# Moving the softmax normalisation of three attentions from VectorE to GpSimd, reading the half maxima as one operand, and swapping two of PE's small uses

## The chip, the cores and the metric

The program runs on one core of one Trainium2 (trn2) chip, as a single launch. The metric is the device time in microseconds (us). Five engines matter: PE (TensorE, matmuls), DVE (VectorE), ACT (ScalarE), POOL (GpSimd), and SP, which only issues the loads and stores here. They run side by side, each takes its own instructions in the order in which they are written, and they wait for each other through semaphores.

## The reference

Two batches of 1024 tokens with 128 features go through eight residual sublayers, each on a layer norm of the running x. Four of the sublayers are attentions with 16 heads of 64. The first (`a0`) has no mask, and its keys and values are shared by the heads; the second (`a1`), the third (`a2`, latent) and the fourth (`a3`, with biases) are causal. The others are quantised linear layers and mixtures of experts. What the change touches is the inner part of an attention:

```python
scores = jnp.einsum('bhsq,bhtq->bhst', q, k)
masked = jnp.where(causal, -jnp.inf, scores)
weights = jax.nn.softmax(masked / jnp.sqrt(jnp.float32(dq)), axis=-1)
out = jnp.einsum('bhst,bhtv->bhsv', weights, v)
return jnp.einsum('bsf,df->bsd', cat, w_o)
```

## The kernel before

**Phases.** `build` runs the phases one after another. `stream_phase` holds `a0` and `a1` in one stream (with the quantised layer between them spread over it), `latent_phase` is `a2`, and `attention_phase` is `a3`. The norms, `moe_phase` and `final_phase` are phases of their own. The change touches `stream_phase` and `attention_phase`, whose inner code is the same but for its bookkeeping.

**Items, steps, units.** An item is a pair of heads and a batch: 16 items in each of `a0`, `a1`, `a3`. An item has two halves of 512 queries (s = 0, 1), each called a unit. A step is one block of 128 keys against one half: 8 + 8 steps per item in `a0`, and 4 + 8 = 12 steps in a causal item (steps 0 to 3 are s = 0, steps 4 to 11 are s = 1; widths shrink on the diagonal). Scores of a step come with keys on the partitions, so the softmax sum over keys is a sum over blocks, made on POOL, and a matmul with ones.

**What one step does.** `scores(g)` on PE: q times k, minus the row maximum (a matmul with `pick`), into one of two buffers of 2 PSUM banks. `exps(g)` on ACT writes the probabilities. `add_up(g)` on POOL adds them into `a.sums`; it skips the first block of a unit, and for the second it waits for PE's `mix_step` of the first. `mix_step(g)` on PE, two steps behind (LAG = 2), multiplies with the values.

**Row maxima, ten steps ahead** (LEAD = 10). `chunk(c)` on PE writes approximate scores of 128 queries against up to 512 keys into the single buffer `chunk_ps`, and `row_max(c)` on DVE reduces it. `chunk(c)` waits for `row_max(c - 1)` (`maxed`), since there is only this one buffer. For more than 512 keys there are two half maxima per query, in `half_max`, of which DVE takes the minimum (they are negated) into `neg_max`.

**Small uses.** One PSUM bank, `small`, is used in turn by everything else on PE. The table `when` gives for each item the step at which each use stands: q, k and v projections, `top` (transpose of `neg_max`, taken by ACT into `max_row`), `total` (ones times `a.sums`, taken by ACT into `a.total`), and `out` (output projection of `a.mixed`, added to `y_t` by DVE). In a causal item each of the 12 steps has exactly one use. PE works in iterations of two steps:

```python
for g in range(BEGIN, LAST, 2):
    chunk(g + LEAD); scores(g); scores(g + 1); chunk(g + 1 + LEAD)
    the use of step g; mix_step(g - 2); mix_step(g - 1); the use of step g + 1
```

**From total to out.** After `total` at step t of a unit, DVE does four `invert` (reciprocals of 128 columns each) at steps t + 1 to t + 4, and `normalise` at step t + 5, ahead of the reciprocal of the same step: `a.mixed` = `a.mixed_raw` times `a.inverse`, 128x512 each. `out` follows. There is one `a.inverse` and one `a.mixed`. So the first `invert` of a unit waits until the unit before has been normalised (semaphore `normed`), and ACT's copy into `a.total` waits for the fourth reciprocal of the unit before (`inverted`). On DVE a step g is: `row_max(g + LEAD)`, then `normalise`, then `invert`, then pieces of the quantised layer; on POOL it is `add_up(g - 1)`, then the rounding copies of q and k (`round_off`).

**Lines.** In the trace of before: `stream_phase`: scores L979, L982, L987; chunk L1003, L1009; mix L1022; total L1057; out L1061; exps L1111; row_max L1194; minimum L1201; reciprocals L1214; normalise L1222; quantised layer L1237 to L1306; POOL's copies L1351 and sums L1361. `attention_phase`: row_max L687, minimum L694, reciprocals L707, normalise L715, sums L772. `latent_phase` already normalises on POOL (L1694).

Of the kernel before, what the change touches and what calls it, by code (L numbers as in the profile page):

```python
# [27 lines left out]
P = 128  # L28
# [18 lines left out]
QUARTERS = 4  # L47
# [330 lines left out]
def attention_phase(nc, m, a, tag, dram, after, causal, biased=False, shared=False):  # L378
# [5 lines left out]
    with phase(nc) as (ctx, new_sem):  # L384
# [48 lines left out]
        if causal:  # L433
            when = {("top", 0): -6, ("top", 1): 2, ("total", 0): 7, ("out", 0): 13, ("total", 1): 15, ("out", 1): 22}
            when |= {("q", 0): -15, ("q", 1): -12}
            if not shared:
                when |= {("k", 0): -16, ("k", 1): -13, ("v", 0): -8, ("v", 1): -7}
        else:
            when = {("top", 0): -2, ("top", 1): 6, ("total", 0): 11, ("out", 0): 18, ("total", 1): 19, ("out", 1): 26}
            when |= {("q", 0): -15, ("q", 1): -12}  # L440
# [231 lines left out]
        def _(dve):  # L672
            v = nc.vector

            def row_max(c):
                i, (t, part, lo, hi) = c // NS, chunks[c % NS]
                s = t // TPG
                dve.wait_ge(chunked, c + 1)
                if split_max[s]:
                    out = a.half_max[:, part, t % TPG, :]  # L680
                    if part == 0 and t % TPG == 0 and unit(i, s) > 0:
                        dve.wait_ge(max_ready, unit(i, s))
                else:
                    out = a.neg_max[:, s, t % TPG, 0:P:HD]
                    if t % TPG == 0 and i >= 1:
                        dve.wait_ge(small_mm, use_of["top", i - 1, s] + 1)
                last = v.tensor_reduce(out, chunk_ps[:, :, 0:hi - lo], AX.X, ALU.max, negate=True)  # L687
                last.then_inc(maxed, 1)
                if c % NS == last_chunk[s]:
                    if split_max[s]:  # L690
                        if i >= 1:
                            dve.wait_ge(small_mm, use_of["top", i - 1, s] + 1)
                        dve.wait_ge(maxed, c + 1)
                        v.tensor_tensor(a.neg_max[:, s, :, 0:P:HD], a.half_max[:, 0], a.half_max[:, 1], ALU.min)\  # L694
                            .then_inc(max_ready, 1)
# [37 lines left out]
            inverts_at, norms_at = {}, {}  # L733
            for i in range(ITEMS):
                for s in range(2):
                    at = i * NS + when["total", s] + 1
                    for quarter in range(QUARTERS):
                        inverts_at[at + quarter] = (i, s, quarter)
                    norms_at[at + QUARTERS] = (i, s)
            for g in range(BEGIN, LAST + 1):  # L740
                if 0 <= g + LEAD < TOTAL:
                    row_max(g + LEAD)
                if g in norms_at:
                    normalise(*norms_at[g])
                if g in inverts_at:
                    invert(*inverts_at[g])
# [5 lines left out]
        def _(pool):  # L752
# [53 lines left out]
def stream_phase(nc, m, a, dram, after):  # L806
# [6 lines left out]
    with phase(nc) as (ctx, new_sem):  # L813
# [74 lines left out]
        def when(i):  # L888
            if layer_of(i)["causal"]:
                at = {("top", 0): -6, ("top", 1): 2, ("total", 0): 7, ("out", 0): 13, ("total", 1): 15, ("out", 1): 22,  # L890
# [286 lines left out]
        def _(dve):  # L1177
# [3 lines left out]
            def row_max(c):  # L1181
# [15 lines left out]
                if ends and split:  # L1197
# [3 lines left out]
                    v.tensor_tensor(a.neg_max[:, s, :, 0:P:HD], a.half_max[:, 0], a.half_max[:, 1], ALU.min)\  # L1201
# [13 lines left out]

            def normalise(i, s):
                u = unit(i, s)
                dve.wait_ge(inverted, QUARTERS * (u + 1))
                dve.wait_ge(mixed_out, u + 1)
                if u >= 1:  # L1220
                    dve.wait_ge(small_mm, use_of["out", (u - 1) // 2, (u - 1) % 2] + 1)
                v.tensor_tensor(a.mixed[:], a.mixed_raw[:, u % 2, :], a.inverse[:], ALU.mult).then_inc(normed, 1)  # L1222
# [85 lines left out]
            inverts_at, norms_at = {}, {}  # L1308
            for i in range(ITEMS):
                for s in range(2):  # L1310
                    at = begins[i] + when(i)["total", s] + 1
                    for quarter in range(QUARTERS):
                        inverts_at[at + quarter] = (i, s, quarter)
                    norms_at[at + QUARTERS] = (i, s)
# [7 lines left out]
            for g in range(BEGIN, LAST + 1):  # L1322
# [6 lines left out]
                if g in norms_at:  # L1329
                    normalise(*norms_at[g])  # L1330
                if g in inverts_at:
                    invert(*inverts_at[g])
# [4 lines left out]
        def _(pool):  # L1337
# [24 lines left out]

            for g in range(BEGIN, LAST + 1):
                if 0 <= g - 1 < TOTAL and step(g - 1)[2] > 0:
                    add_up(g - 1)
                for n, kind, i, part in uses_at.get(g, ()):
# [648 lines left out]
```

## Time and profile before

| | |
|---|---|
| median of 3 runs | 2778.26 us (2777.01 to 2779.09) |
| the profiled execution's own time | 2777.25 us |
| its span | 2775.5 us |
| PE busy | 2530.6 us (91%) |
| PE weight loads | 1243.0 us (45%) |
| DVE busy | 1736.8 us (63%) |
| ACT busy | 1134.6 us (41%) |
| POOL busy | 1237.8 us (45%) |
| mean granted PE clock | 0.945 of full |

The span is what the hardware profiler saw of one execution on the core; the execution's own time is 1.75 us longer, and is what the runs report. Roughly, by the trace: `stream_phase` runs from 45 to 1465 us, `latent_phase` from 1525 to 1880 us, `attention_phase` from 2050 to 2665 us. The shares are averages over all phases. A busy PE is not a PE at its peak, since matmuls overlap; an idle time in front of a PE row, with the engine that ended it, is time in which PE had nothing to run.

### The profile page before, as it was taken

The numbers are of one execution on the slowest core, as the hardware profiler recorded it, in microseconds if no ns is written. First come the engines' busy times: TensorE is split into PE (matmuls) and PEld (weight loads), VectorE is DVE, ScalarE is ACT, GpSimd is POOL, SyncE is SP. The second block draws the span as 40 slices with busy tenths as digits, with TensorE's granted clock in tenths as the row PEclk, the third lists the DMA queues.
The fourth block names the chain that finished last, engine by engine and source line by source line (L and its number), as shares of the span: only waits on it lengthen the run. The fifth ranks groups of instructions, "written<-read, shape, count | busy, mean of one in ns | idle before, by whom it ended". The sixth has DMA issues, their size and how long they took to land. (4 is left out here: it accounts for less than half of the span.)

```text
span 2775.5 us, 47142 instructions
## 1 busy us (share of the span) xinstructions
PE 2530.6 (91%) x19425; PEld 1243.0 (45%) x19425; DVE 1736.8 (63%) x2244; ACT 1134.6 (41%) x1454; POOL 1237.8 (45%) x810
## 2 busy tenths in 40 slices
PE   4999999889999999999994799998869999999968
PEld 2333344333334444444442466665434444444433
DVE  2677767777765766666657467775434666666653
ACT  1444444434444434444441244444214444444422
POOL 2677777666775444555550000000003555555510
PEclk9999999999999999999995699999868999999969
DMA  4000000000000000000000100000000000000000
GB/s 104 1 1 1 1 1 0 1 1 1 1 1 10 1 1 1 1 1 1 1 1 0 32 3 3 3 3 2 0 1 1 1 1 1 1 1 1 1 1 16
DMA packets 19321, 13.99 MB, mean 5 GB/s; under 512 B 3234, under 2 KB 17954, under 8 KB 18979
## 3 DMA queue, kind: packets, MB, share of 16 engines
q1 hardware_dynamic: 19106, 10.97, 1.6%
q8 instruction: 155, 2.54, 0.4%
q14 instruction: 60, 0.48, 0.1%
HBM read 9.39 MB, written 1.57 MB: 4 GB/s over the span
## 5 line engine op out<-in xcount | busy, mean ns | idle before, releaser
L1361 POOL TENSOR_TENSOR sums<-sums,p 128x1024 f32<-128x1024 f32 (+3 forms) x384 | 815.2, 2123 | 389.9 <-PE ps L1022 342.6
L1194 DVE TENSOR_REDUCE half_max<-ps 128x2 f32<-128x1024 f32 (+3 forms) x384 | 440.2, 1146 | 334.9 <-PE ps L1003 322.4
L1111 ACT ACTIVATE p<-ps 128x1024 f32<-128x1024 f32 (+3 forms) x384 | 347.8, 917 | 228.3 <-PE ps L982 163.3
L979 PE MATMUL ps<-q,k 64*128 64x512 f32 (+3 forms) x1792 | 428.0, 556 | 0.0
L772 POOL TENSOR_TENSOR sums<-sums,p 128x1024 f32<-128x1024 f32 (+3 forms) x160 | 276.9, 1731 | 196.1 <-PE ps L545 179.5
L1022 PE MATMUL ps<-p,v 128*64 128x512 f32 (+3 forms) x1536 | 343.8, 562 | 0.0
L982 PE MATMUL ps<-max_row,pick 64*128 64x512 f32 (+3 forms) x896 | 327.2, 726 | 0.0
L1214 DVE RECIPROCAL inverse<-total 128x128 f32<-128x128 f32 x256 | 240.0, 940 | 17.0 <-ACT total L1147 13.2
L1003 PE MATMUL ps<-k_near,q_near 64*128 64x512 f32 (+2 forms) x896 | 201.0, 445 | 51.8 <-DVE half_max L1194 51.7
L687 DVE TENSOR_REDUCE half_max<-ps 128x2 f32<-128x1024 f32 (+3 forms) x128 | 129.2, 1010 | 122.7 <-PE ps L526 107.5
L1003 PEld LDWEIGHTS ps<-k_near,q_near 64*128 64x128 f32 x896 | 85.9, 188 | 265.0 <-issue 157.2
L1578 ACT ACTIVATE p<-ps 128x2048 f32<-128x2048 f32 (+1 forms) x80 | 136.6, 1707 | 161.3 <-PE ps L1483 90.5
L979 PEld LDWEIGHTS ps<-q,k 64*128 64x128 f32 x1792 | 162.9, 187 | 57.1 <-issue 42.1
L1022 PEld LDWEIGHTS ps<-p,v 128*64 128x64 f32 x1536 | 98.0, 139 | 193.5 <-issue 127.1
L1631 DVE TENSOR_REDUCE quarter_max<-ps 128x2 f32<-128x1024 f32 (+3 forms) x128 | 128.3, 1012 | 60.3 <-PE ps L1507 34.8
L502 PE MATMUL ps<-q,k 64*128 64x512 f32 (+3 forms) x768 | 164.8, 507 | 0.0
L611 ACT ACTIVATE p<-ps 128x1024 f32<-128x1024 f32 (+3 forms) x160 | 118.6, 767 | 66.1 <-PE ps L510 49.5
L707 DVE RECIPROCAL inverse<-total 128x128 f32<-128x128 f32 x128 | 119.6, 940 | 15.8 <-ACT total L652 12.3
L982 PEld LDWEIGHTS ps<-max_row,pick 64*128 64x128 f32 x896 | 85.9, 188 | 90.2 <-issue 85.2
L1694 POOL TENSOR_TENSOR mixed<-mixed_raw,inverse 128x256 f32<-128x256 f32 x32 | 23.3, 728 | 229.5 <-DVE inverse L1649 229.5
L505 PE MATMUL ps<-max_row,pick 64*128 64x512 f32 (+3 forms) x384 | 122.1, 632 | 0.0
L1111 ACT ACTIVATE sums<-ps 128x1024 f32<-128x1024 f32 x64 | 65.6, 1025 | 128.6 <-PE ps L982 109.8
(260 smaller groups left out, 3990.5 us busy)
## 6 DMA issues: line engine op xcount, KB each, us to landing
q_w<-in_wq SPq DMA_DIRECT2D x3, 512.0 KB
o_w<-in_wo SPq DMA_DIRECT2D x3, 512.0 KB
k_w<-in_wk SPq DMA_DIRECT2D x2, 512.0 KB
v_w<-in_wv SPq DMA_DIRECT2D x2, 512.0 KB
out<-x SPq DMA_DIRECT2D x4, 256.0 KB, 2.9
scratch<-in_wq_t SPq DMA_DIRECT2D x1, 512.0 KB, 5.4
scratch<-in_w_out SPq DMA_DIRECT2D x1, 512.0 KB, 7.6
gate<-in_gate SPq DMA_DIRECT2D x1, 320.0 KB
```

Source lines behind the costliest of these rows:

```text
L502: nc.tensor.matmul(out[:, head, 0:width], a.k[rows, key_slot(i, 3), k * P:(k + 1) * P], a.q[rows, i % 3, s * BANK + lo:(s + 1) * BANK], st ...
L687: last = v.tensor_reduce(out, chunk_ps[:, :, 0:hi - lo], AX.X, ALU.max, negate=True)
L772: pool.tensor_tensor(sums, sums, probabilities(g)[:, :, lo:BANK], ALU.add).then_inc(summed, 1)
L979: nc.tensor.matmul(out[:, head, 0:width], a.k[rows, owner(i) % 3, k * P:(k + 1) * P], a.q[rows, i % 3, s * BANK + lo:(s + 1) * BANK], star ...
L982: last = nc.tensor.matmul(out[:, head, 0:width], a.pick[rows, :], a.max_row[rows, s, lo:BANK], start=False, stop=not diagonal)
L1003: last = nc.tensor.matmul(chunk_ps[:, head, 0:hi - lo], a.q_near[rows, i % 2, t * P:(t + 1) * P], a.k_near[rows, owner(i) % 2, lo:hi], sta ...
L1022: last = nc.tensor.matmul(mix[rows, lo:BANK], a.v[:, owner(i) % 2, k, value_columns(i, head)], probabilities(g)[:, head, lo:BANK], start=k ...
L1111: act.activation(probabilities(g)[:, :, lo:BANK], score[g % 2][:, :, 0:BANK - lo], ACT.Exp)\
L1194: last = v.tensor_reduce(out, chunk_ps[:, :, 0:hi - lo], AX.X, ALU.max, negate=True)
L1214: v.reciprocal(a.inverse[:, cols], a.total[:, cols]).then_inc(inverted, 1)
L1361: pool.tensor_tensor(sums, sums, probabilities(g)[:, :, lo:BANK], ALU.add).then_inc(summed, 1)
L1578: act.activation(probs[:, g % SLOTS, :, 0:width(s, n)], score[:, :, 0:width(s, n)], ACT.Exp)\
```

## The change

Three things change, in both phases.

1. The minimum of the half maxima is a `tensor_reduce` over one operand (a rearranged view of `half_max`) instead of a `tensor_tensor` of its two halves.
2. `normalise` moves from DVE to POOL, with the same three waits. It stands at the same step, total + 5, after `add_up(g - 1)` and ahead of `round_off`.
3. In causal items `total` of s = 0 goes from step 7 to step 6, and `top` of s = 0 from step -6 (which is step 6 of the item before) to step -5. They swap places. The reciprocals of s = 0 move with the total, to steps 7 to 10. The fourth reciprocal of the unit before stands at step 19, which is step 7 of the next item, so a step may now hold two, and the table of them holds lists.

```diff
         if causal:
-            when = {("top", 0): -6, ("top", 1): 2, ("total", 0): 7, ("out", 0): 13, ("total", 1): 15, ("out", 1): 22}
+            when = {("top", 0): -5, ("top", 1): 2, ("total", 0): 6, ("out", 0): 13, ("total", 1): 15, ("out", 1): 22}
...
                         dve.wait_ge(maxed, c + 1)
-                        v.tensor_tensor(a.neg_max[:, s, :, 0:P:HD], a.half_max[:, 0], a.half_max[:, 1], ALU.min)\
+                        v.tensor_reduce(a.neg_max[:, s, :, 0:P:HD],
+                                        a.half_max[:].rearrange("p a t h -> p t h a"), AX.X, ALU.min)\
                             .then_inc(max_ready, 1)
...
-            def normalise(i, s):
-                u = unit(i, s)
-                dve.wait_ge(inverted, QUARTERS * (u + 1))
-                dve.wait_ge(mixed_out, u + 1)
-                if u >= 1:
-                    dve.wait_ge(small_mm, use_of["out", (u - 1) // 2, (u - 1) % 2] + 1)
-                v.tensor_tensor(a.mixed[:], a.mixed_raw[:, u % 2, :], a.inverse[:], ALU.mult).then_inc(normed, 1)
...
                     for quarter in range(QUARTERS):
-                        inverts_at[at + quarter] = (i, s, quarter)
-                    norms_at[at + QUARTERS] = (i, s)
+                        inverts_at.setdefault(at + quarter, []).append((i, s, quarter))
...
                     row_max(g + LEAD)
-                if g in norms_at:
-                    normalise(*norms_at[g])
-                if g in inverts_at:
-                    invert(*inverts_at[g])
+                for one in inverts_at.get(g, ()):
+                    invert(*one)
...
+            def normalise(i, s):
+                u = unit(i, s)
+                pool.wait_ge(inverted, QUARTERS * (u + 1))
+                pool.wait_ge(mixed_out, u + 1)
+                if u >= 1:
+                    pool.wait_ge(small_mm, use_of["out", (u - 1) // 2, (u - 1) % 2] + 1)
+                pool.tensor_tensor(a.mixed[:], a.mixed_raw[:, u % 2, :], a.inverse[:], ALU.mult).then_inc(normed, 1)
+
+            norms_at = {}
+            for i in range(ITEMS):
+                for s in range(2):
+                    norms_at.setdefault(i * NS + when["total", s] + QUARTERS + 1, []).append((i, s))
             for g in range(BEGIN, LAST + 1):
                 if 0 <= g - 1 < TOTAL and step(g - 1)[2] > 0:
                     add_up(g - 1)
+                for one in norms_at.get(g, ()):
+                    normalise(*one)
```

`invert` itself, with its wait for `normed`, is as it was.

**How the order moves on DVE.** A causal item of `stream_phase`, around its steps 5 to 8, in the kernel before. The brackets name the semaphores waited for; semaphores are reused from phase to phase, and most names in the brackets are those of a former use, but `normed_stream` is this phase's `normed`.

```order
L1214 RECIPROCAL inverse<-total 128x128
L1194 TENSOR_REDUCE half_max<-ps 128x2 [waits vchain0]
L1214 RECIPROCAL inverse<-total 128x128
L1194 TENSOR_REDUCE half_max<-ps 128x2 [waits vchain0]
L1222 TENSOR_TENSOR mixed<-mixed_raw,inverse 128x512 [waits w_in,mixed_out_stream,inverted_stream]
L1214 RECIPROCAL inverse<-total 128x128 [waits normed_stream,zeroed]
L1194 TENSOR_REDUCE half_max<-ps 128x2 [waits vchain0]
```

The same place in the changed kernel:

```order
L1219 RECIPROCAL inverse<-total 128x128
L1198 TENSOR_REDUCE half_max<-ps 128x2 [waits vchain0]
L1219 RECIPROCAL inverse<-total 128x128
L1219 RECIPROCAL inverse<-total 128x128 [waits normed_stream,zeroed]
L1198 TENSOR_REDUCE half_max<-ps 128x2 [waits vchain0]
```

Before, the reduction of step 8 and DVE's own normalise stand ahead of the reciprocal that waits for `normed`. Now that reciprocal follows the fourth one of the unit before directly, ahead of the reduction of step 8.

**How it moves on POOL.** The same causal item, from the sums of steps 5, 6 and 7 (the `x3`) on, before:

```order
L1361 TENSOR_TENSOR sums<-sums,p 128x1024 x3
L1351 CAST k_near<-k 128x512
L1361 TENSOR_TENSOR sums<-sums,p 128x1024
L1351 CAST q_near<-q 128x512
```

and in the changed kernel:

```order
L1355 TENSOR_TENSOR sums<-sums,p 128x1024 x3
L1363 TENSOR_TENSOR mixed<-mixed_raw,inverse 128x512
L1345 CAST k_near<-k 128x512
L1355 TENSOR_TENSOR sums<-sums,p 128x1024
```

The normalise of the unit before stands behind the three sums of steps 5 to 7.

## Rows read from the trace of the kernel before

**Rows 1.** The page's first part: busy time of each engine.

```profile
PE 2530.6 (91%) x19425; PEld 1243.0 (45%) x19425; DVE 1736.8 (63%) x2244; ACT 1134.6 (41%) x1454; POOL 1237.8 (45%) x810
```

**Rows 2.** Timeline of PE, steady causal item: start us, us, instruction, [idle before].

```profile
1199.84 1.03 PE L1022 MATMUL ps<-p,v 128*64 128x512 f32 x4
1200.70 1.03 PE L1057 MATMUL ps<-sums,ones 128*64 128x512 f32 x4
1201.66 0.50 PE L1003 MATMUL ps<-k_near,q_near 64*128 64x512 f32 x2
...
1204.13 0.36 PE L1003 MATMUL ps<-k_near,q_near 64*128 64x256 f32 x2
...
1210.30 0.44 PE L1003 MATMUL ps<-k_near,q_near 64*128 64x384 f32 x2 [0.26 <-DVE half_max L1194]
...
1233.97 0.66 PE L1053 MATMUL ps<-ident,neg_max 128*128 128x128 f32 x4
...
1235.47 1.03 PE L1022 MATMUL ps<-p,v 128*64 128x512 f32 x4
```

**Rows 3.** Timeline of POOL, the same item.

```profile
1200.17 7.63 POOL L1361 TENSOR_TENSOR sums<-sums,p 128x1024 f32<-128x1024 f32 x3 [7.74 <-PE ps L1022]
```

**Rows 4.** Timeline of DVE, the same item.

```profile
1203.34 2.24 DVE L1222 TENSOR_TENSOR mixed<-mixed_raw,inverse 128x512 f32<-128x512 f32 x1
1205.68 0.95 DVE L1214 RECIPROCAL inverse<-total 128x128 f32<-128x128 f32 x1
1206.55 0.63 DVE L1194 TENSOR_REDUCE half_max<-ps 128x2 f32<-128x512 f32 x1
...
1209.02 1.23 DVE L1194 TENSOR_REDUCE half_max<-ps 128x2 f32<-128x1024 f32 x1 [0.99 <-PE ps L1003]
```

**Rows 5.** Timeline of POOL, the same three sums in an item with DVE quieter.

```profile
1050.49 7.35 POOL L1361 TENSOR_TENSOR sums<-sums,p 128x1024 f32<-128x1024 f32 x3 [12.10 <-PE ps L1022]
```

**Rows 6.** Groups by line and form: count, busy us, mean ns, idle before.

```profile
L1222 DVE TENSOR_TENSOR mixed<-mixed_raw,inverse 128x512 f32<-128x512 f32 x64 | 90.0, 1406 | 0.1
...
L1201 DVE TENSOR_TENSOR neg_max<-half_max 128x8 f32<-128x8 f32 x48 | 47.1, 981 | 4.9
...
L1361 POOL TENSOR_TENSOR sums<-sums,p 128x512 f32<-128x512 f32 x32 | 41.1, 1283 | 8.3 <-ACT p L1111 3.8
...
L694 DVE TENSOR_TENSOR neg_max<-half_max 128x8 f32<-128x8 f32 x16 | 2.8, 173 | 1.6
```

**Rows 7.** Timeline of PE: three of its stalls in the quantised stretches.

```profile
571.63 0.79 PE L1003 MATMUL ps<-k_near,q_near 64*128 64x512 f32 x2 [2.50 <-DVE half_max L1194]
...
931.24 0.80 PE L1003 MATMUL ps<-k_near,q_near 64*128 64x512 f32 x2 [4.38 <-DVE half_max L1194]
...
974.75 0.69 PE L1003 MATMUL ps<-k_near,q_near 64*128 64x384 f32 x2 [2.05 <-DVE half_max L1194]
```

**Rows 8.** Windows of 2 us behind them; PEclk is third from the end.

```profile
574.00:576.00 2.00, 2.00 (x8) 0.38 (x4) 1.95 (x3) 0.10 (x1) 1.86 (x2) 0.73 0.00 0
...
940.00:942.00 2.00, 2.00 (x8) 0.81 (x8) 0.08 (x1) 0.59 (x1) 0.00 (x0) 0.92 0.00 0
...
980.00:982.00 2.00, 2.00 (x6) 0.50 (x2) 0.00 (x0) 0.00 (x0) 0.00 (x0) 0.68 0.00 0
```

**Rows 9.** Waits of PE for DVE, 450 to 700 us: total us, times, longest.

```profile
PE ps L1003 <- DVE half_max L1194: 19.0, 10, 5.0
```

**Rows 10.** The same, 880 to 1100 us.

```profile
PE ps L1003 <- DVE half_max L1194: 11.6, 9, 4.4
```

**Rows 11.** The same in `attention_phase`, 2050 to 2620 us.

```profile
PE ps L526 <- DVE half_max L687: 8.7, 19, 1.3
...
PE ps L526 <- DVE neg_max L687: 2.5, 3, 1.1
```

**Rows 12.** Timeline of POOL, last four sums of a unit of `a0`.

```profile
275.50 10.15 POOL L1361 TENSOR_TENSOR sums<-sums,p 128x1024 f32<-128x1024 f32 x4
```

**Rows 13.** Timeline of PE, the next `out` of the same place.

```profile
287.73 1.12 PE L1061 MATMUL ps<-mixed,o_w 128*128 128x512 f32 x2
```

More of the change, by code:

```diff
@@ L732, in _ @@
             dve.wait_ge(cleared, 1)
-            inverts_at, norms_at = {}, {}
+            inverts_at = {}
             for i in range(ITEMS):
@@ L889, in when @@
             if layer_of(i)["causal"]:
-                at = {("top", 0): -6, ("top", 1): 2, ("total", 0): 7, ("out", 0): 13, ("total", 1): 15, ("out", 1): 22,
+                at = {("top", 0): -5, ("top", 1): 2, ("total", 0): 6, ("out", 0): 13, ("total", 1): 15, ("out", 1): 22,
                       ("q", 0): -15, ("q", 1): -12}
@@ L1200, in row_max @@
                     dve.wait_ge(maxed, c + 1)
-                    v.tensor_tensor(a.neg_max[:, s, :, 0:P:HD], a.half_max[:, 0], a.half_max[:, 1], ALU.min)\
+                    v.tensor_reduce(a.neg_max[:, s, :, 0:P:HD],
+                                    a.half_max[:].rearrange("p a t h -> p t h a"), AX.X, ALU.min)\
                         .then_inc(max_ready, 1)
@@ L1214, in invert @@
                 v.reciprocal(a.inverse[:, cols], a.total[:, cols]).then_inc(inverted, 1)
[L1216 to L1222, printed above, removed]
             def add_out(n, i, s):
@@ L1306, in quantise_step @@
                 return v.tensor_tensor(split(even), split(z), wide(scale), ALU.mult)
-            inverts_at, norms_at = {}, {}
+            inverts_at = {}
             for i in range(ITEMS):
@@ L1312, in _ @@
                     for quarter in range(QUARTERS):
-                        inverts_at[at + quarter] = (i, s, quarter)
-                    norms_at[at + QUARTERS] = (i, s)
+                        inverts_at.setdefault(at + quarter, []).append((i, s, quarter))
             def take_small(g):
@@ L1328, in _ @@
                     take_small(g - 1)
[L1329 to L1332, printed above, removed]
+                for one in inverts_at.get(g, ()):
+                    invert(*one)
                 for work in dve_at.get(g, ()):
@@ L1361, in add_up, with normalise @@
                 pool.tensor_tensor(sums, sums, probabilities(g)[:, :, lo:BANK], ALU.add).then_inc(summed, 1)
+            def normalise(i, s):
+                u = unit(i, s)
+                pool.wait_ge(inverted, QUARTERS * (u + 1))
+                pool.wait_ge(mixed_out, u + 1)
+                if u >= 1:
+                    pool.wait_ge(small_mm, use_of["out", (u - 1) // 2, (u - 1) % 2] + 1)
+                pool.tensor_tensor(a.mixed[:], a.mixed_raw[:, u % 2, :], a.inverse[:], ALU.mult).then_inc(normed, 1)
+            norms_at = {}
+            for i in range(ITEMS):
+                for s in range(2):
+                    norms_at.setdefault(begins[i] + when(i)["total", s] + QUARTERS + 1, []).append((i, s))
             for g in range(BEGIN, LAST + 1):
@@ L1365, in _ @@
                     add_up(g - 1)
+                for one in norms_at.get(g, ()):
+                    normalise(*one)
                 for n, kind, i, part in uses_at.get(g, ()):
```

## The prediction

> **What bounds the kernel now.** I read the page's engine line first [rows 1]: PE is busy 91% of the span and no other engine above 63%, so the time is PE's work plus the holes in it. The timeline of PE in a steady causal item [rows 2] shows matmuls back to back, with one hole of 0.26 us. The list of PE's waits gives the rest: PE waits for DVE's row maxima 19.0 us and 11.6 us in the two stretches into which the quantised layer is woven [rows 9, 10], and 8.7 + 2.5 us in `attention_phase` [rows 11]. So freeing DVE can give back only some tens of us in 2777, and whatever makes PE wait in every item weighs more.
>
> **What DVE gains.** The minimum of 8 numbers per partition takes 981 ns on average in `stream_phase` (48 of them) and 173 ns in `attention_phase`; the normalise takes 1406 ns (64 of them) [rows 6]. The excess is waiting: the normalise of 2.24 us [rows 4] lies wholly inside POOL's three sums [rows 3]. The Trainium skill (SBUF — State Buffer, "Who interferes with whom") says that a VectorE instruction with two SBUF inputs and a GpSimd one that reads SBUF exclude each other for a whole instruction, and that a `tensor_reduce` never contends; the trace agrees, and by that rule alone the whole change is a gain. In rows: 48 x (0.981 - 0.173) = 39 us for the minima and 90 us for the normalises leave DVE in the stream. PE gets only what it waited for:
> - Second quantised stretch: the 11.6 us [rows 10], and the slow clock behind its stalls. PE resumed at 931.24 and 974.75 [rows 7], and by the mixed windows the clock was full again at 940.3 and 981.3 [rows 8] (a window at 0.92 of full was at half, 1.2 GHz, for 0.32 us of its 2). That is 9.1 + 6.5 = 15.6 us at half, 7.8 lost. Together 19 us; I take 16, as the layer's pieces now add about 3 us to the new wait below.
> - First quantised stretch: of the 19.0 us [rows 9] most comes from the layer's own two-operand instructions, which stay. I take 8, between 0 and 19.
> - `attention_phase`: the hole of 0.26 us per item is PE having too little between two chunks (the reduction between them starts at 1209.02, the chunk at 1210.30 [rows 2, 4]), and stays: 16 x 0.26 = 4.2 of the 11.2 us [rows 11]. I take 4 of the rest, between 0 and 7.
> - The two phase ends lie open: there a normalise of 1.28 us takes the place of one of about 0.7 us, +1 us in all.
>
> Sum so far: -27 us. The normalise on POOL is priced by its sum of the same form, 1283 ns for 128x512 [rows 6].
>
> **Where that normalise must be covered.** In `a0` it comes behind the last sum of a unit, which ends at 275.50 + 10.15 = 285.65 [rows 12]; with 1.28 it ends at 286.9, and PE wants `out` at 287.73 [rows 13]. Covered, by 0.8 us. In `a0` the reciprocals that wait for it stand four steps later: nothing.
>
> **The new wait.** In a causal item it is otherwise. `a.inverse` is one buffer, so the first reciprocal of s = 0 waits until the unit before (s = 1 of the item before) is normalised. Before, both were DVE's, and the normalise stood just ahead. Now that reciprocal stands at step 7 and the normalise at POOL's step 8, behind `add_up(7)`. The first of POOL's three sums there (steps 5, 6, 7) cannot start before `mix_step(4)`. DVE is in order, so the reduction of chunk 18 (step 8) is queued behind the blocked reciprocal, and PE's chunk 19 waits for that reduction, the chunk buffer being single. `scores(10)` and everything else of PE is behind chunk 19. Count from T, when PE starts `mix_step(5)` (1199.84 [rows 2]):
> - POOL starts the sums at T + 0.33 (1200.17 [rows 3]). Three take 7.63 us with DVE's normalise among them, 7.35 us without [rows 5]: T + 7.7.
> - Normalise 1.28: T + 9.0.
> - Reciprocal, 1205.68 to the next instruction's start at 1206.55 [rows 4]: 0.87. T + 9.9.
> - Reduction of chunk 18, and chunk 19 behind it, 1.28 as above: T + 11.15.
> - PE's own work: `mix_step(5)` 0.86 (1200.70 - 1199.84), then the transpose `top` that has moved here, 0.6 (at 1233.97 it shows 0.66 with its tail), where `total` took 0.96, then chunk 18 and the scores of steps 8 and 9, 1204.13 - 1201.66 = 2.47 [rows 2]. Chunk 19 is wanted at T + 3.9.
>
> So PE stands for 7.2 us. It happens at each start of a causal item that has a unit before it: 16 in `a1` (its first item follows `a0`) and 15 in `a3`, 31 in all. 31 x 7.2 = 223 us. Bounds 6.9 (a handoff or two shorter) to 7.6 (sums as in [rows 3]): 214 to 236.
>
> **The clock behind it.** Each of the stalls shown was followed by half clock: it lasted 3.5, 9.1 and 6.5 us after PE had resumed [rows 7, 8] (at 571.63 full again by 575.1). Half of that is lost: 1.7 to 4.5 us. The one at nearly the same place of an item, 974.75, gives 3.2; I take 2.8, since long matmuls follow our stall as at 571.63, where it was shortest. 31 x 2.8 = 87 us, bounds 53 and 140.
>
> The move of `total` and `top` costs PE nothing: they swap, and the ACT copies of both are long done when PE needs them. But it is what puts the reciprocal at step 7. POOL's later work moves by 1.28 us and then has a long idle time (7.74 before the next sums [rows 3]): nothing.
>
> **Sum**: 223 + 87 - 27 = +283 us on the profiled execution's 2777.25: **3060 us**. The median of the runs is 1 us above that execution, within the rounding.
>
> **Rivals.**
> - *Faster* (0.04): POOL has normalised before DVE comes to the reciprocal, or DVE's later work hides the wait. Then the gains stand alone, with some of the stalls in `a0` gone as well: 2777 - 27 = 2750 us. For it: 129 us of DVE time go. Against it: POOL would need to be done 7.2 us sooner, and it starts behind a matmul of the same item. It decides from the point where sums, normalise, reciprocal and reduction together take less than 3.6 us. This is also the outcome that the skill's rule on the shared port alone would give.
> - *The wait without the clock* (0.08): PE loses the 223 us and keeps its full clock. 2777 + 223 - 27 = 2973 us. Against it: all three stalls shown were followed by half clock.
> - *The clock stays low far longer* (0.05): 15 us after each stall rather than 5.6 (twice 2.8), since these are longer than any in the trace. 7.5 us x 31 = 232: 2777 + 223 + 232 - 27 = 3205 us.
> - *POOL is late for `out` in `a0` too* (0.03): the 0.8 us there are too few and PE waits 1 us in each of 32 units: 3060 + 32 = 3092 us.
> - *The minimum on DVE waits as before* even with one operand: the change does not do what it says. It costs a few us of the gains and lies inside the range.
> - *No change to speak of* (0.01).
>
> **Numbers.** Forecast 0.79. Its bounds are 2777 + 214 + 53 - 50 = 2994 and 2777 + 236 + 140 - 10 = 3143. The range 2985 to 3135 holds most of it, and the `out` rival. A measurement of this kernel can tell 0.2% (5.5 us) from no change: faster 0.04, same 0.01, slower 0.95.
>
> **What would show it.** PE's waits should list chunk <- row maximum with about 31 entries of some 7 us, in both phases. On DVE two reciprocals should stand together in each causal item, the second with an idle time of 6 to 8 us before it that ends with POOL's normalise, and the reduction of chunk 18 behind it. The causal steady stretches should fall from PE 99% busy and clock 1.00 to some 80% and 0.9 or less, while those of `a0` stay as they are. The minimum should take under 0.3 us everywhere, and POOL's normalise 1.28 us. I am wrong if the causal item (35.6 us from 1199.84 to 1235.47 [rows 2]) keeps its length, or if the idle time before the second reciprocal is below 3 us.

## The result, and the profile after

| | before | after |
|---|---|---|
| median | 2777.64 us (2775.51 to 2779.09) | 3007.43 us (3005.99 to 3014.08) |
| the profiled execution's own time | 2777.25 us | 3007.11 us |
| its span | 2775.5 us | 3005.4 us |
| mean granted PE clock | 0.945 | 0.912 |

The changed kernel takes 1.0833 times as long, 95% interval 1.0814 to 1.0851: 230 us slower. The forecast was 3060 us, the range 2985 to 3135.

The first part of the page, after (compare [rows 1]):

```profile
PE 2580.0 (86%) x19425; PEld 1257.3 (42%) x19425; DVE 1568.2 (52%) x2148; ACT 1137.2 (38%) x1454; POOL 1342.2 (45%) x906
```

DVE is 169 us less busy, as it was meant to be, and PE's share fell from 91% to 86%: 425 us of the span without a matmul, where there were 245. The list of PE's waits says what it waits for (engine, line, releaser: us in total, times, longest):

```profile
PE ps L1007 <- DVE half_max L1198: 123.7, 49, 7.5
PE ps L526 <- DVE half_max L687: 105.3, 33, 7.2
...
PE ps L574 <- POOL mixed L770: 10.0, 3, 5.5
PE ps L1065 <- POOL mixed L1363: 10.0, 3, 5.5
```

Chunks waiting for row maxima took 52 us in `stream_phase` before and 9 us in `attention_phase` [rows 11]; now it is 124 and 105. A steady causal item, timeline of PE (compare [rows 2]):

```profile
1242.00 0.58 PE L1007 MATMUL ps<-k_near,q_near 64*128 64x256 f32 x2 [6.88 <-DVE half_max L1198]
...
1275.33 1.03 PE L1026 MATMUL ps<-p,v 128*64 128x512 f32 x4
1276.29 0.66 PE L1057 MATMUL ps<-ident,neg_max 128*128 128x128 f32 x4
1276.88 0.50 PE L1007 MATMUL ps<-k_near,q_near 64*128 64x512 f32 x2
...
1286.39 0.58 PE L1007 MATMUL ps<-k_near,q_near 64*128 64x256 f32 x2 [6.88 <-DVE half_max L1198]
```

The same place on POOL (compare [rows 3]):

```profile
1275.66 7.32 POOL L1355 TENSOR_TENSOR sums<-sums,p 128x1024 f32<-128x1024 f32 x3 [8.01 <-PE ps L1026]
1282.94 1.26 POOL L1363 TENSOR_TENSOR mixed<-mixed_raw,inverse 128x512 f32<-128x512 f32 x1
```

and on DVE (compare [rows 4]):

```profile
1274.02 0.94 DVE L1219 RECIPROCAL inverse<-total 128x128 f32<-128x128 f32 x1
1284.31 0.95 DVE L1219 RECIPROCAL inverse<-total 128x128 f32<-128x128 f32 x1 [9.35 <-POOL mixed L1363]
1285.17 1.16 DVE L1198 TENSOR_REDUCE half_max<-ps 128x2 f32<-128x1024 f32 x1
```

Read the three together, from the bottom. PE's chunk at 1286.39 waited for the reduction at 1285.17. That one was behind the reciprocal at 1284.31, and that one waited 9.35 us for POOL's normalise, which POOL could only begin after three sums of 7.32 us. The sums began 0.33 us after PE started the `mix_step` at 1275.33. The item, from stall to stall, takes 44.39 us; it took 35.63 (1199.84 to 1235.47).

Of those 8.76 us PE stands for 6.88. The rest is the clock. Windows of 2 us around the stall that ends at 1242.00 (PEclk is third from the end):

```profile
1238.00:1240.00 2.00, 0.00 (x0) 0.00 (x0) 0.09 (x1) 0.00 (x0) 1.81 (x2) 0.72 0.00 0
1240.00:1242.00 2.00, 0.00 (x1) 0.00 (x1) 2.00 (x3) 0.00 (x0) 0.00 (x0) 0.50 0.00 0
1242.00:1244.00 2.00, 2.00 (x8) 0.95 (x8) 2.00 (x3) 0.00 (x0) 0.00 (x0) 0.50 0.03 8
1244.00:1246.00 2.00, 2.00 (x5) 0.53 (x6) 0.31 (x1) 0.60 (x1) 0.59 (x2) 0.57 0.00 0
1246.00:1248.00 2.00, 2.00 (x8) 0.44 (x4) 0.00 (x0) 0.00 (x0) 2.00 (x2) 1.00 0.01 4
```

PE resumed at 1242.00 at half clock (1.2 GHz) and got the full one back (2.4 GHz) at about 1245.7: 3.7 us at half, some 1.9 lost. The half clock had begun at about 1238.9 (a mean of 0.72 from 1238 to 1240 is 1.1 us at half). So 3.1 of its 6.8 us lay inside the stall, where they cost nothing.

**Where the 230 us are.** Both traces cut at the same five places of the program, us from one to the next:

| stretch | before | after | difference |
|---|---|---|---|
| start to the first causal row maximum (`a0`) | 822.2 | 797.5 | -24.7 |
| to the last `out` of `a1` | 642.2 | 761.7 | +119.5 |
| to the first chunk of `a3` (with `a2`) | 603.2 | 608.6 | +5.4 |
| to the last `out` of `a3` | 594.8 | 726.1 | +131.3 |
| to the end | 113.1 | 111.5 | -1.6 |

So the whole loss stands in the two causal phases, 251 us of it, and `a0` has become faster.

### The profile page after: what moved, and what is told of

The parts are those of the page before. It is cut to its first block and busy times, and to the rows that moved or that the text cites. A ratio compares the mean times of both kernels' runs of the same rounds, so it can differ in the third digit from the quotient of the medians.

```text
span 3005.4 us, 47142 instructions
## 1 busy us (share of the span) xinstructions
PE 2580.0 (86%) x19425; PEld 1257.3 (42%) x19425; DVE 1568.2 (52%) x2148; ACT 1137.2 (38%) x1454; POOL 1342.2 (45%) x906
## 5 line engine op out<-in xcount | busy, mean ns | idle before, releaser
L1355 POOL TENSOR_TENSOR sums<-sums,p 128x1024 f32<-128x1024 f32 (+3 forms) x384 | 804.7, 2096 | 368.3 <-PE ps L1026 326.6
L762 POOL TENSOR_TENSOR sums<-sums,p 128x1024 f32<-128x1024 f32 (+3 forms) x160 | 272.1, 1700 | 206.6 <-PE ps L545 190.1
L1026 PE MATMUL ps<-p,v 128*64 128x512 f32 (+3 forms) x1536 | 347.3, 567 | 0.0
L986 PE MATMUL ps<-max_row,pick 64*128 64x512 f32 (+3 forms) x896 | 326.4, 725 | 0.0
L526 PE MATMUL ps<-k_near,q_near 64*128 64x512 f32 (+3 forms) x384 | 86.4, 446 | 107.7 <-DVE half_max L687 105.3
L752 POOL CAST k_near<-k 128x512 fp32r<-128x512 f32 x32 | 19.6, 611 | 246.3 <-ACT k L633 246.3
L545 PE MATMUL ps<-p,v 128*64 128x512 f32 (+3 forms) x640 | 128.0, 515 | 0.0
```

The lines of the kernel that those rows point to most:

```text
L762: pool.tensor_tensor(sums, sums, probabilities(g)[:, :, lo:BANK], ALU.add).then_inc(summed, 1)
L986: last = nc.tensor.matmul(out[:, head, 0:width], a.pick[rows, :], a.max_row[rows, s, lo:BANK], start=False, stop=not diagonal)
L1026: last = nc.tensor.matmul(mix[rows, lo:BANK], a.v[:, owner(i) % 2, k, value_columns(i, head)], probabilities(g)[:, head, lo:BANK], start=k ...
L1355: pool.tensor_tensor(sums, sums, probabilities(g)[:, :, lo:BANK], ALU.add).then_inc(summed, 1)
```

## The experiments

The theory: one reciprocal buffer, shared by DVE and POOL, makes DVE wait for POOL; everything behind it on DVE waits too, and with it PE. The rivals: the swap of `total` and `top` itself costs the time; or the normalise is simply too slow on POOL; or the wait is there and something else sets its length.

### Two reciprocal buffers

The units take turns in two buffers. Nothing else differs from the changed kernel (the same in both phases).

```diff
-                    if u >= 1:
-                        dve.wait_ge(normed, u)
-                v.reciprocal(a.inverse[:, cols], a.total[:, cols]).then_inc(inverted, 1)
+                    if u >= 2:
+                        dve.wait_ge(normed, u - 1)
+                v.reciprocal((a.inverse if u % 2 == 0 else a.inverse2)[:, cols], a.total[:, cols]).then_inc(inverted, 1)
...
+        a.inverse2 = m.scratch[:, 7680:8192]
```

> The changed kernel with a second buffer for the reciprocals (units take turns), so the first reciprocal of a unit waits for the unit before the last to be normalised, no longer for the last. Same instructions, same places. Theory A (that one wait of VectorE for GpSimd's normalise, 6.9 us of PE in each of 31 items, with 3.7 us of half clock behind each): all of it goes, and what is left is the gain of a freed VectorE, some 45 us by the stage ends of the two traces: 2725 to 2745 us. Rival B (GpSimd is too loaded, or out comes late, whatever the reciprocals wait for): 2900 us or more. Rival C (the swap of total and transpose itself makes PE wait): 2850 us or more.

Measured: 2756.53 us (2753.71 to 2760.95), 0.9928 of before (0.9913 to 0.9943). The entire loss goes with this one wait, 251 us of it, and what is left is 21 us faster than the kernel before. PE's waits:

```profile
PE ps L1007 <- DVE half_max L1198: 32.7, 38, 3.2
PE ps L574 <- POOL mixed L770: 10.9, 5, 5.6
PE ps L1065 <- POOL mixed L1363: 10.8, 5, 5.6
```

Chunks wait 33 us instead of 124, and the normalise is still POOL's and the table still the new one. Neither is the cause by itself.

### The same wait, reached by moving the normalise

One buffer as in the changed kernel, but the normalise of s = 1 in causal items stands ahead of the three sums, at total + 2.

```diff
-                    norms_at.setdefault(begins[i] + when(i)["total", s] + QUARTERS + 1, []).append((i, s))
+                    norms_at.setdefault(begins[i] + when(i)["total", s] + (2 if s and layer_of(i)["causal"] else QUARTERS + 1), []).append((i, s))
```

> The changed kernel with the single buffer, but GpSimd's normalise of the second unit of a causal item three steps earlier, ahead of the three sums of steps 5 to 7 of the next item instead of behind them. Theory A: the normalise ends about 1 us after the fourth reciprocal, before VectorE's next reduction is due; PE's stall goes: 2725 to 2750 us. Rivals B and C as before: GpSimd does exactly the same work and the swap is in, so 2850 us or more.

Measured: 2760.27 us, 0.9939 of before (0.9921 to 0.9957). With POOL's order alone changed the loss is gone as well. So it was the normalise's place behind the sums, not its 1.26 us. But both runs end above what I expected of them (up to 2745 and up to 2750 us): the rest of the change gives about 20 us, not the 45 or so that I had counted on. The cause of the loss does not hang on that.

### The old table

The changed kernel with the table of before, so that the first reciprocal of s = 0 stands at step 8, behind the reduction of chunk 18.

```diff
-    when = {("top", 0): -5, ("top", 1): 2, ("total", 0): 6, ("out", 0): 13, ("total", 1): 15, ("out", 1): 22}
+    when = {("top", 0): -6, ("top", 1): 2, ("total", 0): 7, ("out", 0): 13, ("total", 1): 15, ("out", 1): 22}
```

> The changed kernel with the old table: total at step 7, transpose at -6, so the first reciprocal of a unit stands at step 8 behind the reduction of chunk 18 instead of ahead of it. Theory A: chunk 19 runs, VectorE is blocked as long, and now chunk 20 waits. PE wants it 4.4 us later than chunk 19, and the chain ends 0.6 us sooner: a stall of about 2 us per item, 62 us, with 0 to 60 us of half clock: 2790 to 2860 us. Rival C (the swap): all of it goes, about 2735 us. Rival B: still near 3000 us.

Measured: 2842.45 us, 1.0231 of before (1.0214 to 1.0248). The steady causal item, PE:

```profile
1245.22 0.50 PE L1007 MATMUL ps<-k_near,q_near 64*128 64x512 f32 x2 [1.85 <-DVE half_max L1198]
1247.15 0.45 PE L1007 MATMUL ps<-k_near,q_near 64*128 64x384 f32 x2 [0.37 <-DVE half_max L1198]
```

and DVE:

```profile
1243.66 0.95 DVE L1219 RECIPROCAL inverse<-total 128x128 f32<-128x128 f32 x1 [5.42 <-POOL mixed L1363]
```

DVE still waits for POOL, but 5.42 us rather than 9.35, and it has handed PE one reduction more before it does. PE stands for 1.85 us instead of 6.88. The clock stays full as well (PEclk is third from the end):

```profile
1200.00:1280.00 80.00, 75.55 (x539) 36.45 (x535) 39.75 (x47) 35.33 (x51) 47.94 (x35) 1.00 0.00 1
```

The steady item of `a1` takes 37.65 us, and none of that is slow clock. (In the last attention 6 of 13 items have 3.4 us at half clock.) The move of the normalise makes the wait; the swap puts it where nothing covers it, and there the stall is followed by half clock every time. Without the swap the kernel is 65 us slower than before, with it 230.

### One more product on POOL

The changed kernel with a second product of the same form ahead of the normalise, into unused columns, for s = 1 in causal items.

```diff
                 if u >= 1:
                     pool.wait_ge(small_mm, use_of["out", (u - 1) // 2, (u - 1) % 2] + 1)
+                if s and layer_of(i)["causal"]:
+                    pool.tensor_tensor(a.spare, a.mixed_raw[:, u % 2, :], a.inverse[:], ALU.mult)
```

> The changed kernel, with one more product of 128x512 on POOL, into unused columns, ahead of the normalise of s = 1 in causal items. Theory A (PE's stall is the chain sums, normalise, reciprocal, reduction, all of it uncovered): each of the 29 stalls grows by the 1.26 us of one such product, 6.88 to 8.1 us, and the two phase ends by 2.5 us each: 3007 + 37 + 5 = 3049, between 3040 and 3065 with the clock, which should stay low about as long behind each. Theory B (the wait is set by something else, such as ACT's copy of the total or PE's own order, and POOL is only named): 3007 to 3015. Theory C (the time at half clock grows with the stall): 3049 plus another 0.5 to 1 us per stall, 3065 to 3080.

Measured: 3050.04 us (3048.56 to 3054.64), 42.6 us more than the changed kernel. POOL and PE in the steady item:

```profile
1289.75 7.32 POOL L1357 TENSOR_TENSOR sums<-sums,p 128x1024 f32<-128x1024 f32 x3 [8.01 <-PE ps L1028]
1297.04 1.26 POOL L1366 TENSOR_TENSOR scratch<-mixed_raw,inverse 128x512 f32<-128x512 f32 x1
1298.25 1.26 POOL L1367 TENSOR_TENSOR mixed<-mixed_raw,inverse 128x512 f32<-128x512 f32 x1
```

```profile
1301.70 0.58 PE L1009 MATMUL ps<-k_near,q_near 64*128 64x256 f32 x2 [8.10 <-DVE half_max L1200]
...
1347.21 0.58 PE L1009 MATMUL ps<-k_near,q_near 64*128 64x256 f32 x2 [8.10 <-DVE half_max L1200]
...
1393.84 0.58 PE L1009 MATMUL ps<-k_near,q_near 64*128 64x256 f32 x2 [8.10 <-DVE half_max L1200]
```

The stall grew by 1.22 us for 1.26 us on POOL: the chain is uncovered from end to end, as the theory has it. The first item shown takes 45.51 us, 9.88 more than before: 8.10 are the stall and 1.78 the clock. The second takes 46.63, of which 2.9 are the clock. In the last attention the two lengths alternate (46.12 on average); half clock lasts about 3.5 us after PE has resumed in the shorter items and 5.7 in the longer. So the clock's part did grow a little with the stall on average, though not in every item. The sum, from the spans: 28 stalls grew (the first of `a1` waits for a normalise of `a0`, which is not doubled), 28 x 1.22 = 34; 2 x 2.4 at the two phase ends; what is left of the 46.4 us that `a1` and the last attention took more, some 7, goes with the clock; the rest of the program took 3.5 less. Together 43.

### The minimum alone

The kernel before, with nothing but the one-operand minimum.

```diff
-    v.tensor_tensor(a.neg_max[:, s, :, 0:P:HD], a.half_max[:, 0], a.half_max[:, 1], ALU.min)\
+    v.tensor_reduce(a.neg_max[:, s, :, 0:P:HD], a.half_max[:].rearrange("p a t h -> p t h a"), AX.X, ALU.min)\
```

> The kernel before with only the minimum of the half maxima read as one operand; normalise stays on VectorE. The minimum should take 0.17 us each (0.98 on average before) and PE should get back a part of its waits in the first attention: 5 to 25 us: 2752 to 2773 us. A rival, that what VectorE waits for moves on to its next two-operand instruction: no change, 2777 us.

Measured: 2758.41 us, 0.9936 of before (0.9921 to 0.995): 19 us faster, by itself. `a0` takes 12.6 us less, the last attention the same 594.8 us. `a1` takes 4.6 us less, with the very same waits of PE for row maxima (15.1 us) and 10 us less at half clock: that part is the clock's, and what changed the clock there is not shown. Groups of DVE, by form (compare [rows 6]):

```profile
L1222 DVE TENSOR_TENSOR mixed<-mixed_raw,inverse 128x512 f32<-128x512 f32 x64 | 99.6, 1556 | 0.1
...
L1201 DVE TENSOR_REDUCE neg_max<-half_max 128x8 f32<-128x16 f32 x48 | 8.3, 173 | 5.2
```

The minimum takes 173 ns where it took 981. What it waited for is plain from DVE and POOL in `a0`. Before, the minimum ends as POOL's third sum does:

```profile
273.41 1.63 DVE L1201 TENSOR_TENSOR neg_max<-half_max 128x8 f32<-128x8 f32 x1
267.63 7.37 POOL L1361 TENSOR_TENSOR sums<-sums,p 128x1024 f32<-128x1024 f32 x3 [3.76 <-PE ps L1022]
```

and with one operand it runs beside a sum:

```profile
270.11 0.17 DVE L1201 TENSOR_REDUCE neg_max<-half_max 128x8 f32<-128x16 f32 x1
264.33 7.37 POOL L1361 TENSOR_TENSOR sums<-sums,p 128x1024 f32<-128x1024 f32 x3 [3.76 <-PE ps L1022]
```

Of the 32 minima of `a0` before, 31 start inside a sum of POOL and take 1.41 us on average; 15 of the 16 in `a1` meet no sum and take 174 ns, two operands or not. The normalise did not get better but longer, 1556 ns for 1406, all of it in `a0` (1.32 to 1.64 us on average; in `a1` it stays at 1.48).

### The normalise alone

Two buffers, the new table, the normalise on POOL, but the old minimum (the edit above, undone).

> The change with two reciprocal buffers, but with the old two-operand minimum: the move of the normalise and the swap alone, without the new wait. With both parts it was 2756.5 us, the minimum alone gave 2758.4 against 2777.2. Theory A (each part frees DVE from waiting beside GpSimd, and PE takes only what it waited for, so the parts overlap): 2760 to 2772, well short of two separate gains. Theory B (the move of the normalise gives nothing, all of the 21 us is the minimum's): 2774 to 2782. If the old minimum costs here what it cost in the kernel before (19 us): 2775.

Measured: 2773.72 us, 0.9992 of before (0.9983 to 1.0001). Theory B holds for the total, just below its range: no gain that can be told from nothing, although DVE is 116 us less busy. But the total hides two parts. `a1` takes 635.1 us, 7 less than before, with 9.0 us of waits for row maxima instead of 15.1; the last attention takes 599.6, 5 more, and it loses them at its end (see the phase ends below). `a0` takes 822.1 us, to 0.1 us the time of before, and both its stretches without and with the quantised layer show the very waits of before:

```profile
PE ps L1006 <- DVE half_max L1197: 3.9, 8, 0.5
```

```profile
PE ps L1006 <- DVE half_max L1197: 19.0, 10, 5.0
```

(80 to 450 us and 450 to 700 us; before, 3.9 and 19.0 [rows 9].) The parts do not add up in `a0`: minimum alone -12.6 us, normalise alone -0.1, both together -21.0 (two buffers) to -24.7 (the changed kernel). What PE waited for in the steady part was a reduction behind the slow minimum; while that stays, an emptier DVE elsewhere is worth nothing in `a0`. Once it is gone, the normalise matters in the quantised stretch: 19.0 us of waits fall to 14.7 with the minimum alone and to 9.7 with both.

### The table, with and without the normalise on DVE

First: two buffers, the change, the old table (the table edit above on top of the two buffers).

> Two reciprocal buffers, normalise on POOL, new minimum, but the old table (first total at step 7, first transpose at -6). Theory A (the swap costs PE nothing, as predicted; the 4 to 5 us that the last attention lost against the kernel before come from the normalise on POOL, which delays the sums and the outputs): 2754 to 2759, as with the new table (2756.5). Theory B (the swap itself costs those us, through a later neg_max transpose or a later first reduction): 2747 to 2752, and the last attention takes 595 us rather than 599.5.

Measured: 2760.67 us (2756.32 to 2767.14), 0.9946 of before (0.9931 to 0.996), beside 0.9928 (0.9913 to 0.9943) with the new table. The intervals overlap, and the last attention took the same to 1 us. The median lies 2 us above theory A's range and far above theory B's: the swap costs nothing here, nor does it clearly gain.

Second: the minimum, the new table and two buffers, with the normalise left on DVE.

> Kernel before plus new minimum plus the new table, with two reciprocal buffers so that the table can stand, the normalise staying on DVE. Theory A (swap costs nothing): 2756 to 2761, like the minimum alone (2758.4), last attention 595 us. Theory B (swap costs 4 to 5 us in each causal phase): 2763 to 2770, last attention 599 us.

Measured: 2775.99 us, 0.9998 of before (0.9989 to 1.0007), 18 us behind the minimum alone. The swap does cost, and more than I had thought possible, where DVE still normalises. The profiled execution is the slowest of the twelve (2784.18 us), 8 us above the median, so only the stretch inside the last attention is read from it. PE's waits there have an entry that no other kernel has:

```profile
PE ps L556 <- DVE y_t L720: 12.4, 13, 1.0
```

and DVE shows why, in the steady item:

```profile
2299.07 0.94 DVE L707 RECIPROCAL inverse<-total 128x128 f32<-128x128 f32 x1
2299.93 0.89 DVE L687 TENSOR_REDUCE half_max<-ps 128x2 f32<-128x768 f32 x1
2300.92 1.82 DVE L715 TENSOR_TENSOR mixed<-mixed_raw,inverse 128x512 f32<-128x512 f32 x1
2302.67 0.68 DVE L720 TENSOR_TENSOR y_t<-y_t,ps 128x512 f32<-128x512 f32 x1
```

PE's `out` of the unit before is done at 2300.8, but its sum into `y_t`, which frees the `small` bank, now stands behind the normalise of s = 0, and PE's next projection waits 0.96 us for it, in 13 items. The last attention, from its first to its last `out`, took 545.2 us against 529.7; the 12.4 us of waits are most of that. So the swap belongs with the normalise on POOL, given two buffers.

### POOL in `a0` only

The minimum, the table of before, one buffer; the normalise goes to POOL in the items without a mask and stays on DVE in the causal ones.

```diff
-                if g in norms_at:
+                if g in norms_at and layer_of(norms_at[g][0])["causal"]:
                     normalise(*norms_at[g])
...
+            norms_at = {begins[i] + when(i)["total", s] + QUARTERS + 1: (i, s) for i in range(ITEMS) for s in range(2)
+                        if not layer_of(i)["causal"]}
```

> Kernel before plus new minimum, the normalise on POOL only in the items without a mask (a0), on DVE in the causal ones, old table, one reciprocal buffer. By the stages of the earlier runs a0 gains 8 us more than with the minimum alone (801 against 810), and the causal phases stay as with the minimum alone, less 4 us once for the first causal item, whose first reciprocal waits for POOL: 2749 to 2755, the fastest so far. If the gain of a0 was not the normalise's: 2758.

Measured: 2756.41 us, 0.9926 of before (0.9914 to 0.9938). `a0` took 797.3 us, 12.3 less than with the minimum alone, so its gain is the normalise's too. It needs no second buffer and no new table; 1.4 us more than expected.

### The phase ends on DVE

Two buffers and the change, with the last three normalises of each causal phase back on DVE.

```diff
                 for one in norms_at.get(g, ()):
-                    normalise(*one)
+                    if unit(*one) < 2 * ITEMS - 3:
+                        normalise(*one)
...
+                if g in ends_at:
+                    normalise(*ends_at[g])
```

> The change with two reciprocal buffers (2756.5 us), and the last three normalises of each causal phase back on DVE, where no sums and no chunks are left to hide them. Theory A (at the end of a causal phase the normalise on POOL costs 4.3 us: 2.5 + 1.9 + 5.5 us of waits for POOL in the changed kernel against 0.2 + 2.8 + 4.9 in the one before, plus the work between): 2748, between 2745 and 2752, and the waits of the output projection for a normalise go back to about 5 us in each phase. Theory B (the last attention is longer for another reason, such as POOL's sums being delayed all along): 2755 to 2758.

Measured: 2754.49 us (2750.14 to 2756.05), 0.9915 of before (0.9901 to 0.9928). It is the fastest median, by 2 us, and its interval overlaps that of four others. The place is as theory A says: from first to last `out` the last attention takes 530.8 us instead of 534.2, and `a1` takes 635.4 instead of 640.8. Together that is 8.8 us, but only 2 arrive, so that the total lies between the two theories; 5.6 went in the stretch between `a1` and `a2` (below).

## Why the prediction was right, and where its sizes were off

**The wait, its place and its chain: right.** From T = 1275.33 the forecast had the sums at T + 0.33, their end at T + 7.7, the normalise's at T + 9.0, the reciprocal's at T + 9.9, the chunk at T + 11.15. Measured: T + 0.33, T + 7.6, T + 8.9, T + 9.8 (the next instruction starts), T + 11.06. The chunk was wanted at T + 4.2, not T + 3.9 (the `mix_step` took 0.96 us, not 0.86, the chunk and the scores behind it 2.63, not 2.47). So the stall is 6.88 us, just below the lower bound of 6.9. The signs named came out too: the steady causal stretches have PE 84% busy and a clock of 0.92 (some 80% and 0.9 or less were forecast). One was wrong: the idle time before the blocked reciprocal is 9.35 us, not 6 to 8. The forecast's own terms give 9.4, from the end of the reciprocal before it, some 0.4 us before T, to T + 9.0. Three runs bear on the cause: two ways of taking the wait away (two buffers, an earlier normalise) give back 251 and 247 us, and one product more in the chain adds its own length.

**The count: 29, not 31.** "16 in `a1` and 15 in `a3`" counted the reciprocals that wait; the groups of DVE do show 16 and 15. But the last item of a phase has no chunks ahead of it, so its blocked DVE holds nothing of PE there. In `a1` PE stands 15 times, eleven of them for 6.88 us, three for 7.12 to 7.47, once (at 1056.02, a piece of the quantised layer) for 8.25; in `a3` 14 times, for 6.88 or 7.16. Together 105.7 + 97.2 = 203 us, where the forecast had 223.

**The clock: 1.9 to 2.2 us a stall, not 2.8.** This is the largest error. The steady items of `a1` are 44.41 long on average (1108.59 to 1508.29, nine of them): 8.78 over 35.63, less 6.88, is 1.90. Those of `a3` are 44.80 (2260.60 to 2843.03, thirteen) where they were 35.67: 9.13 less 6.94 is 2.19. 15 x 1.90 + 14 x 2.19 = 59 us, against 87. The 2.8 was taken between 974.75, the row nearest in place (3.2 us), and 571.63, the one followed by like work (3.5 us at half clock, 1.7 lost); the second was the better guide, and the bounds of 1.7 to 4.5 held. What the forecast lacked is where the half clock begins. At 974.75 it lasted from about 974.4 to 981.3, nearly all of it after PE had resumed; in our stall it is as long, 6.8 us, but begins 3.1 us before PE resumes. Nor does half clock follow every stall, as the three rows chosen suggest: in the kernel before PE waited 2.59 us before a chunk at 545.43, and the clock from 544 to 552 is 1.00.

**The gains.** In `a0` I took 8 us and nothing for its steady part: it was 24.7. In the quantised stretch it was 15.3 (the same `out` to the same `out`, 474.1 to 694.9 us before, 467.1 to 672.6 after): the waits fell by 9.4 (19.0 to 9.6) and the clock behind them rose (windows 500 to 600 and 600 to 700: 0.96 and 0.97 before, 1.00 and 0.98 after). The other 9.4 came in the steady part. It had a hole of 0.51 us in each item, behind the slow minimum, that I had passed over (3.9 us of waits from 80 to 450 us before, 0.3 after), and its items went from 45.5 to 44.8 us. `out` in `a0` stayed covered, as forecast. The second quantised stretch is taken as what is left of `a1`: 119.5 - 105.7 - 28.5 for the clock - 3.6 for the phase end (below) = -18, against -16. But without the stalls, with two buffers, `a1` gains only 1.4, or some 5 without its phase end: most of the 16 was not there to be had by freeing DVE. That the changed kernel shows more may be because the layer's waits fall into the stalls and their slow clock; no run here tests that. In `attention_phase` 4 us were forecast and about 1 came (97.2 + 30.7 + 4.5 = 132.4 against 131.3).

**The phase ends: +8 us together, not +1.** From the last chunk of the phase to its last `out` PE took 35.88 us in `a1` and 34.98 in `a3` before, and 39.45 in both after: +3.6 and +4.5. PE at the end of `a3`, before:

```profile
2647.91 1.13 PE L574 MATMUL ps<-mixed,o_w 128*128 128x512 f32 x2
...
2651.51 1.10 PE L574 MATMUL ps<-mixed,o_w 128*128 128x512 f32 x2 [0.17 <-DVE mixed L715]
2655.44 1.08 PE L570 MATMUL ps<-sums,ones 128*64 128x512 f32 x4 [2.83 <-POOL sums L772]
2661.44 2.04 PE L574 MATMUL ps<-mixed,o_w 128*128 128x512 f32 x2 [4.93 <-DVE mixed L715]
```

and after:

```profile
2877.50 2.05 PE L574 MATMUL ps<-mixed,o_w 128*128 128x512 f32 x2 [2.54 <-POOL mixed L770]
...
2884.38 1.10 PE L574 MATMUL ps<-mixed,o_w 128*128 128x512 f32 x2 [1.94 <-POOL mixed L770]
2886.26 1.08 PE L570 MATMUL ps<-sums,ones 128*64 128x512 f32 x4 [0.78 <-DVE y_t L713]
2892.89 2.04 PE L574 MATMUL ps<-mixed,o_w 128*128 128x512 f32 x2 [5.55 <-POOL mixed L770]
```

I had priced one normalise, 1.28 for 0.7. What counts is that the first of these three stands behind POOL's last sums, with no work left on PE to cover them; the second and third are delayed with it. The last run above takes that back.

**The sum.** 203 (stalls) + 59 (clock) - 24.7 (`a0`) - 18 (second quantised stretch) - 1 (`a3`) + 8 (phase ends) + 5.4 - 1.6 (the stretches between and behind) = 230. That it meets the 229.9 us of the spans shows nothing, since the 18 and the 1 are what was left over. The forecast's 223 + 87 - 27 = 283 was 53 us too high: 20 from count and stall, 28 from the clock, and 5 from its -27, which came out as -32 (the gains 16 better, the phase ends 7 worse, the stretches between and behind 4 worse).

**The Trainium skill's rule.** The Trainium skill (SBUF — State Buffer, "Who interferes with whom") says that a `tensor_reduce` on VectorE does not contend with GpSimd. The trace agrees: 173 ns for the same 8 numbers, also in the 30 minima of `a0` that start inside a sum of POOL, against 1.41 us with two operands. That by this rule the whole change is a gain (2750 us) is what the kernel with two buffers shows, at 2756.5; the rule is silent on the wait that decided it.

**The rivals.** *Wait without clock* (2973 us) fell by the 2-us windows; *clock low far longer* (3205) by the same. *POOL late in `a0`* fell: `a0` is faster, and PE's three waits for POOL's normalise in `stream_phase` all lie at the end of `a1`. *The minimum waits as before*: 173 ns. *Faster* would have come true with a second buffer.

## What to carry to other kernels

When an instruction moves to another engine, look for every buffer that the two engines now share and ask what stands behind the first instruction that waits for it: a wait of the next writer until the old content has been read, which was free inside one in-order queue, becomes the other engine's whole backlog, and the in-order queue passes it on to work that has nothing to do with it. Count such a wait only where something of the bounding engine still lies behind it, and price its clock by a stall that is followed by like work, counting only the half clock that lies behind the stall. And try parts alone and together: here the minimum gave nearly all of the gain by itself; the normalise gave nothing in `a0` until the minimum was gone; and the swap cost 18 us with the normalise on DVE, nothing with it on POOL and two buffers, and 165 us with it on POOL and one buffer.

## What the runs showed of the hardware that I had not expected

- The price of half clock did not follow the length of the stall. In the steady items of `a1`, stalls of 1.85 us were followed by none (the old table), stalls of 6.88 us by 3.7 to 4.0 us of it, and stalls of 8.10 us (one product more) by 3.4 to 6.7. A part of each slow spell lay inside the stall (3.1 us of the one around 1242.00). In the kernel before, a stall of 2.05 us (at 974.75) was followed by 6.5.
- DVE's two-operand minima and normalises that started inside a sum of POOL all ended only after it: the 31 minima of `a0` by 0.03 us (median), the normalises there by 0.55. A `tensor_reduce` of the same 8 numbers, started inside a sum, took its 173 ns.
- The stretch from the last `out` of `a1` to the first of `a2` is the same code in every kernel here. It took 122.0 to 122.2 us in five of them, 123.4 in one, and 126.3 to 127.8 in the six others (122.0 in the kernel before, 127.8 in the changed one, 127.7 in the one with its phase ends on DVE). The granted clock differs. In the kernel before a spell of some 3 us at full clock, from 1524, fell into the stretch, and the clock came back for good 111 us after the last `out`; in the changed kernel there was no such spell and it came back after 123 us. Four kernels that left `a1` between 1436.3 and 1442.0 us all reached the first `out` of `a2` between 1563.9 and 1564.4. What decides it, no run here shows. A gain of a few us ahead of this stretch may therefore not arrive at the end, and it is the +5.4 us of the table of stretches.
- The normalise on DVE became slower when the minimum became fast: 1406 to 1556 ns on average. In both kernels 26 of the 30 in `a0` start inside a sum of POOL and end 0.55 us after it; with the fast minimum they start earlier in the sum, and so wait longer for its end.
